# A graph network's node update at the end: products in column and row halves of TensorE's array

## The reference, cut to what matters

```python
h = relu(layernorm(x))
message = relu(concat(h[src], h[dst], edge) @ msg_W1 + msg_b1) @ msg_W2 + msg_b2
agg = segment_sum(message, dst)
x = x + relu(concat(agg, h) @ upd_W1 + upd_b1) @ upd_W2 + upd_b2      # the node update
```

## Time and profile before

| | |
|---|---|
| median of 3 runs | 3957.04 us (3954.34 to 3957.98) |
| the profiled execution's own time | 3974.8 us |
| its span | 3973.0 us |
| TensorE busy, whole span | 2800.8 us (70%) |
| mean granted TensorE clock | 0.769 |
| node update, from its first product (3936.58) to the span's end | 36.4 us |

### The profile page before, as it was taken

One profiled execution on the slowest core, in us unless ns is written; L12 is line 12 of the kernel. 1 busy time (PEld: TensorE's weight loads), 2 busy tenths in 40 slices (PEclk: granted clock), 3 DMA queues, 4 the chain that ended last, 5 costly groups with the idle time before them and its releaser, 6 DMA issues.

```text
span 3973.0 us, 102120 instructions
## 1 busy us (share of the span) xinstructions
PE 2800.8 (70%) x37635; PEld 2380.6 (60%) x37635; DVE 1621.9 (41%) x4904; ACT 1292.0 (33%) x3188; POOL 1478.0 (37%) x1462
## 2 busy tenths in 40 slices
PE   2457777677784777777777777777777777777778
PEld 2335555555563666666666666666666666666666
DVE  8735544444556333333333333333333333333333
ACT  0135555454563222222222222222222222222222
POOL 0654444333424334333333333333333333333331
PEclk6668888787886777877777777777777777777778
DMA  1000000000002122112211121221122112112211
GB/s 44 19 18 16 16 16 16 15 15 15 16 10 52 40 40 42 39 38 41 40 39 41 39 40 39 41 40 39 38 42 40 39 39 42 39 38 42 39 39 38
DMA packets 365051, 133.31 MB, mean 34 GB/s; under 512 B 312657, under 2 KB 342455, under 8 KB 364919
## 3 DMA queue, kind: packets, MB, share of 16 engines
q1 hardware_dynamic: 320248, 85.81, 9.9%
q0 software_dynamic: 44672, 45.83, 6.5%
HBM read 123.94 MB, written 7.54 MB: 33 GB/s over the span
## 4 chain that ended last, share of the span: by engine, by line
PE 67%; issue 23%; DVE 5%; another core or an unknown queue 4%; ACT 1%; DVEq 0%; POOL 0%; DMA 0%; PEldq 0%; ACTq 0%; SPq 0%; POOLq 0%
PE psum L1662 13%; PE psum L1651 12%; PE psum L1717 11%; PE psum L1519 7%; PE psum L1551 7%; PE psum L1641 7%; PE psum L1675 3%; PE psum L1699 3%; PE psum L1540 2%; PE psum L1530 1%; ACT hT L1286 1%; DVE Z L957 1%; PE psum L1485 0%; DVE work L834 0%
## 5 line engine op out<-in xcount | busy, mean ns | idle before, releaser
L673 POOL DMA_INDIRECT rows<-a_rows,idx x980 | 973.2, 993 | 1717.8 <-DMA idx<-src_by_tile 1432.9
L1651 PE MATMUL psum<-wb,eoT 128*64 128x64 f32 x6272 | 502.9, 267 | 461.4 <-issue 451.7
L1651 PEld LDWEIGHTS psum<-wb,eoT 128*64 128x64 f32 x6272 | 371.8, 170 | 571.5 <-issue 569.8
L1286 ACT ACTIVATE hT<-psum 128x392 bf16<-128x392 f32 x1152 | 518.8, 503 | 500.6 <-PE psum L1551 285.6
L1662 PE MATMUL psum<-Y,Z 128*128 128x64 bf16 x8820 | 526.4, 235 | 162.5 <-issue 162.4
L673 POOL DMA_INDIRECT rows<-g_rows,idx x416 | 411.7, 990 | 550.4 <-DMA idx<-src_by_tile 430.7
L1551 PE MATMUL psum<-Z,lo_hi 128*128 128x392 f16 x1152 | 419.5, 380 | 259.7 <-issue 169.7
L1662 PEld LDWEIGHTS psum<-Y,Z 128*128 128x128 bf16 x8820 | 465.2, 126 | 219.3 <-issue 200.2
L1519 PE MATMUL psum<-work,hT 128*128 128x192 bf16 x3528 | 513.6, 269 | 15.9 <-issue 13.2
L1356 ACT ACTIVATE Y<-psum 128x512 f16<-128x512 f32 (+1 forms) x392 | 150.0, 435 | 1151.1 <-PE psum L1699 1147.7
L1374 ACT ACTIVATE Y<-psum 128x384 bf16<-128x384 f32 (+1 forms) x588 | 255.6, 439 | 769.6 <-remote 580.9
(11 more groups left out here) (273 smaller groups left out, 2344.7 us busy)
## 6 DMA issues: line engine op xcount, KB each, us to landing
work<-in_edge_attr_dram SPq DMA_DIRECT2D x392, 128.0 KB
Z<-slot_code SPq DMA_DIRECT2D x196, 96.0 KB
rows<-a_rows,idx POOLq DMA_INDIRECT x980
rows<-g_rows,idx POOLq DMA_INDIRECT x416
idx<-src_by_tile SPq DMA_DIRECT2D x197, 2.5 KB, 1.7
wb<-b_rows SPq DMA_DIRECT2D x196, 16.0 KB
g_rows<-Y SPq DMA_DIRECT2D x1, 1600.0 KB, 7.1
a_rows<-Y SPq DMA_DIRECT2D x6, 256.0 KB, 2.3
```

The costliest lines, as they stand in the source:

```text
L673: pool.indirect_dma_start(out=rows[:, k, t, :], out_offset=None, in_=table, in_offset=bass.IndirectOffsetOnAxis(ap=idx[:, k, t:t + 1], axis=0)
L1286: nc.scalar.activation(counts[:, j % 2, :, t * SLOTS:(t + 1) * SLOTS], psum[:, t % 4, 0:KEYS].rearrange("p (h m) -> p h m", m=SLOTS), ACT.Copy
L1651: TT.matmul(psum[half:half + D, 2 + k % 2, t * D:(t + 1) * D], eoT[:, k % 2, t, half:half + D], wb[:, k, :], start=(t == 0), stop=False)
```

## The change

Chunks of 512 nodes are taken in pairs. The hidden features of an even chunk are computed only into rows 0 to 63, those of an odd chunk only into rows 64 to 127, in the same bank; each product uses 64 columns of the weights. The four products of a pair are written as: `w_node` for the even chunk, `w_node` for the odd, `w_agg` for the even, `w_agg` for the odd. ScalarE writes 64 rows by 512 nodes for each chunk. The second products contract the 64 rows that hold the chunk's hidden features, with the unhalved `w_upd2`; a block of the even chunk (rows 0 to 63) and one of the odd (rows 64 to 127) stand in turn, and they write to two different banks. VectorE reads both banks in one instruction. `w_out` and the instruction that made it go. Semaphores rise once for each pair on TensorE. The order is hidden 0, 1, and then in turn one pair of hidden calls two ahead and one pair of output calls, so three hidden pairs stand before the first output.

```diff
-        w_out = sb("w_out", [P, D])
...
-                V.tensor_tensor(Y[:, c:c + m, :], psum[:, 4 + (c // T) % 2, 0:m * D].rearrange("p (b d) -> p b d", d=D),
-                                X[:, c:c + m, :], ALU.add).then_inc(s_u3c, 1)
+                banks = slice(4 + 2 * ((c // T) % 2), 6 + 2 * ((c // T) % 2))
+                if m == T:
+                    V.tensor_tensor(Y[:, c:c + m, :].rearrange("p (a b) d -> p a b d", a=2),
+                                    psum[:, banks, 0:T // 2 * D].rearrange("p a (b d) -> p a b d", d=D),
+                                    X[:, c:c + m, :].rearrange("p (a b) d -> p a b d", a=2), ALU.add).then_inc(s_u3c, 1)
...
-            nc.scalar.activation(w_out[:, :], w_upd2[:, :], ACT.Copy, scale=0.5).then_inc(s_wTc, 1)
...
-                act.wait_ge(s_u2, q + 1)
-                nc.scalar.activation(acc[:, c:c + m], psum[:, q % 4, 0:m], ACT.Relu, bias=b_upd1[:, :]).then_inc(s_u2c, 1)
+                half = slice(q % 2 * D, q % 2 * D + D)
+                act.wait_ge(s_u2, q // 2 + 1)
+                nc.scalar.activation(acc[half, c:c + m], psum[half, (q // 2) % 4, 0:m], ACT.Relu, bias=b_upd1[half, :]
+                                     ).then_inc(s_u2c, 1)
...
-            pe.wait_ge(s_wTc, 7)
+            pe.wait_ge(s_wTc, 6)
...
+            def half_of(q):
+                return slice(q % 2 * D, q % 2 * D + D)
+
+            def hidden(pair):
+                chunks = [(q, min(512, NP - q * 512)) for q in (2 * pair, 2 * pair + 1) if q * 512 < NP]
+                if pair >= 4:
+                    pe.wait_ge(s_u2c, 2 * (pair - 3))
+                for weights, from_, first in ((w_node, hT, True), (w_agg, acc, False)):
+                    for q, m in chunks:
+                        ins = TT.matmul(psum[half_of(q), pair % 4, 0:m], weights[:, half_of(q)], from_[:, q * 512:q * 512 + m],
+                                        start=first, stop=not first)
+                ins.then_inc(s_u2, 1)
+
+            def output(pair):
+                if pair >= 2:
+                    pe.wait_ge(s_u3c, pair - 1)
+                pe.wait_ge(s_u2c, min(2 * pair + 2, -(-NP // 512)))
+                for b in range(HB):
+                    for q in (2 * pair, 2 * pair + 1):
+                        n = q * HB + b
+                        if n < NB:
+                            ins = TT.matmul(psum[:, 4 + 2 * (pair % 2) + q % 2, b * D:(b + 1) * D],
+                                            acc[half_of(q), n * P:(n + 1) * P], w_upd2[half_of(q), :], start=True, stop=True)
+                ins.then_inc(s_u3, 1)
+
+            hidden(0)
+            hidden(1)
+            for pair in range(NPAIR):
+                if pair + 2 < NPAIR:
+                    hidden(pair + 2)
+                output(pair)
```

More of the change, by code:

```diff
@@ L1250, in _ @@
                 dve.wait_ge(s_u3, c // T + 1)
-                V.tensor_tensor(Y[:, c:c + m, :], psum[:, 4 + (c // T) % 2, 0:m * D].rearrange("p (b d) -> p b d", d=D),
-                                X[:, c:c + m, :], ALU.add).then_inc(s_u3c, 1)
+                banks = slice(4 + 2 * ((c // T) % 2), 6 + 2 * ((c // T) % 2))
[3 more added lines that the diff above has]
+                                    X[:, c:c + m, :].rearrange("p (a b) d -> p a b d", a=2), ALU.add).then_inc(s_u3c, 1)
+                else:
+                    V.tensor_tensor(Y[:, c:c + m, :], psum[:, banks.start, 0:m * D].rearrange("p (b d) -> p b d", d=D),
+                                    X[:, c:c + m, :], ALU.add).then_inc(s_u3c, 1)
         @block.scalar
@@ L1739, in _ @@
             HB = 512 // P
[L1741 to L1758, removed]
@@ L1760, in _ @@
-            hidden(0)
[L1761 to L1766, removed]
+            NPAIR = -(-NB // T)
+            def half_of(q):
[9 more added lines that the diff above has]
+                ins.then_inc(s_u2, 1)
```

## The result

The changed kernel takes 3928.82 us (median of 8 runs, 3911.85 to 3935.99) where the kernel before takes 3949.88 (8 runs, 3941.86 to 3960.15): ratio 0.9948, 95% interval 0.9932 to 0.9965, faster by some 21 us (13.8 to 27 by the interval). I had forecast 3945.3 in a range from 3939 to 3955: the sign is right, the time lies outside the range.

What follows compares the result with a forecast made beforehand. TensorE's own work bounds the node update: first products 13.22, second 5.67 and switches 1.8 make 20.7 us against 32.4, 11.7 less. From the median 3957.04 that gives 3945.3, range 3939 to 3955.

Steps and rivals of the forecast that it cites:

- C: Rival (0.07), node update: halves don't run together with 512 fp32 columns, switches come on top; 1.3 us more, 3958.3.
- D: Rival (0.03), node update: granted clock falls; at half all the way the passes double, 7.2 us more than now, 3964.2.
- the slots: First products: passes start in order, one per half at a time, so n passes take n/2 + 1 slots; 13.22 us.
- My own check: Edge loop, line 1651: n/2 + 1 slots give 17 x 0.054 = 0.92 us against 0.93 measured.
- Second products: Output stages: loads of lower and upper 64 rows overlap; 16 passes take 9 slots, 0.95 us; pairs 0 to 5, 5.67.
- B: Rival (0.24), second products: the row halves' loads don't overlap, 1.68 us a pair; 4.4 us more, 3949.7.
- Switches: TensorE in the node update: 9 changes between column and row halves at 0.2 us, 1.8 us in all, bounds 0 to 2.3.
- A: Main case (0.60), node update: both overlaps hold; 3945.3 us, with bounds 3941.8 to 3945.8.
- The cover: Node update: ScalarE stays hidden behind TensorE, and VectorE's late start is covered by 1.8 us.
- E: Rival (0.06), edge loop: moved buffers and shorter ScalarE code lengthen TensorE's waits; at 5%, 3967.9; against: three runs within 3.6 us.
- a drift of the loop: Range: A's and B's 3941.8 to 3949.7, widened by some 3 us on one side, 5 on the other.
- My sign for E: Profile after: up to 3936 us it should be as before; a shift there is E, or its opposite.

Runs made afterwards that it cites:

- the kernels that undo the placement: Two kernels: the one before with w_out behind all other buffers, ratio 0.9998; the changed one with w_out, its copy and wait put back, 3926.29 us, ratio 0.9957.

## Why the prediction was right and wrong

- **What bounds it, right.** TensorE alone set the update's end, and still does. Rivals C and D did not happen: the passes overlap, and the clock was 1.00 throughout in all three profiles of the changed kernel. (Where the update began at half clock in other runs, one of them was the kernel before.)
- **First products: the slots were mis-sized.** "I take it that a pass starts no earlier than the one before it" failed. I had 13.22 us for all of them; measured are 5.37 + 3 x 1.87 + 1.01 = 11.99 with the switches in them. A stage of 8 passes takes 4 slots and a switch, since TensorE starts the other half's pass ahead of three waiting ones. My own check, 0.92 against 0.93 for line 1651, was luck. In the trace of the kernel before the single passes of that line start two by two, 0.003 us apart, every 0.058 us, from the first pair on; one look at that pair shows it:

```profile
3926.95 0.23 PE L1651 MATMUL psum<-wb,eoT 128*64 128x64 f32 x2
```

So the 0.93 was 16 slots of 0.058 and not 17 of the 0.054 that I had scaled from wider passes. The bound of 4 slots was in the working and was the truth.
- **Second products, right in kind.** Loads of the two row halves overlap, as I took from the column halves; B did not happen. 8 slots of 0.112 and a switch make the 1.04; I had 0.95 and 0.2.
- **Switches, right in size:** 0.15 us each instead of 0.2. With the slots the update took 18.1 us and not 20.7: 14.3 us saved, not 11.7, inside A's own bounds.
- **The cover held:** no wait for ScalarE or VectorE that lengthened the chain. TensorE was faster than I had it, and VectorE's slack of 1.8 us shrank to 0.1 (its first add ended at 3898.9, the loads of output 2 began at 3899.05); with closer outputs it is gone.
- **The time, wrong, by 16.5 us** (3945.3 to 3928.8). Of this 2.6 is the slots. 7.2 is the base: I took the median of three runs, 3957.04, while eight runs have 3949.88. The other 6.7 is the part of the first timing's 21 us that is not the update. It is no more than these runs can be off by: the interval, 0.9932 to 0.9965, holds 14.3 us (0.9964), two repetitions gave 11.8 us (ratio 0.9970 of 3943) and 15.5, and the kernels that undo the placement showed no such effect. That it was scatter of the loops is what these numbers suggest; it is not shown, since the first timing can't be taken apart.
- **The step that failed** for the time is "the three runs lie within 3.6 us" under E, and with it the 3 to 5 us for "a drift of the loop" in the range. Single executions of the kernel before lie 37.5 us apart on one chip (3922.98 to 3960.5), and the medians of two chips are 34 us apart (3943.18 and 3977.09). The profiled execution's 3974.8, which I carried along as a difference that the change leaves alone, is above all 35 runs of the one chip and among the 30 of the other (3967.83 to 3987.21); it probably came from a chip like the second. Either way it was the warning, and a range of 16 us around the median of three runs was too narrow. My sign for E, a shift of the profile ahead of the update, came up with 48.6 us and was no sign: in the three profiles of the one changed kernel the update begins at 3887.9, 3909.8 and 3955.3.

## What to carry to other kernels

Where half of TensorE's array does something twice, two half-array streams side by side took little more than half the time of the stage here: 1.87 us instead of 3.44 for first products, 1.04 instead of 1.68 for second ones, switches included, and nothing at all was gained where both streams used the same half. Turns by product were enough for fp32's two passes, and so were runs of four passes (column halves); with runs of eight (row halves) half of the overlap was lost. Each change between column and row halves cost 0.15 us, so stages may be short. And a gain of 0.4% in a straight stretch is read from the chain of that stretch: the median of three whole runs was off by half of the gain, and two chips differed by more than twice the gain.

## What the runs showed of the hardware

**The same program needs 2172 us on one chip and 3943 or 3977 on two others**, and each variant ran near the pace of its chip. The rows of the costliest wait in the edge loop, changed kernel on a slower chip, then the order with fewer switches on the faster (busy, mean ns, idle before):

```profile
L1657 PE MATMUL psum<-wb,eoT 128*64 128x64 f32 x6272 | 513.3, 267 | 482.1 <-issue 475.2
```

```profile
L1657 PE MATMUL psum<-wb,eoT 128*64 128x64 f32 x6272 | 215.7, 222 | 0.0
```

Windows within the same loop, in the same order:

```profile
1300.00:3800.00 2500.00, 1830.25 (x29338) 1640.53 (x29338) 872.52 (x2762) 687.60 (x1843) 912.77 (x923) 0.77 0.20 40
```

```profile
1300.00:2100.00 800.00, 798.95 (x19605) 765.02 (x19602) 565.94 (x1846) 439.81 (x1231) 612.08 (x617) 1.00 0.40 84
```

On the faster chip TensorE never stops and the granted clock is 1.00; on the others it stops again and again, mostly for 0.2 to 0.5 us between passes and now and then for 1, for nothing that the profile shows, and the clock is 0.77 on the mean. By the starts of this line a superblock takes 13.8 us there and 6.5 on the faster chip. The last three superblocks, which are written out and not in the hardware loop, start 6.01 and 4.51 us apart in profiles from every chip, and the node update has its full pace on all of them. What makes the stops I did not find out; here it explains why the scatter sits in the loops, and that the gain of some 14 us is 0.4% on the one and 0.6% on the other.

**The clock at the update's start.** In four of the profiles (the one shown above and all three from the faster chip) it was granted at or near half for the first few us of the update, in the other nine not. It cost 1.6 to 1.8 us, in kernels of either kind. The thinner work just ahead does not tell them apart. The first profile of the kernel before, which kept its full clock, was as thinly busy in the 7.2 us ahead of the update, 4.11 us against 4.09 above:

```profile
3929.30:3936.50 7.20, 4.11 (x118) 3.66 (x114) 1.40 (x5) 1.38 (x4) 0.00 (x0) 1.00 0.01 2
```

What does tell them apart stays open.

**Halves of the array.** The Trainium skill (TensorEngine Tiling, Key Properties) has a change of mode drain TensorE; the trace agrees, at 0.15 us, and the loads of the new mode start only behind the slot of the old one's last pass (they stand idle for 0.81 us). The list in the Trainium skill (TensorE: Matmul & The Clock Gate, The mechanism) lets a weight load overlap running products only where the row group differs; the text above the list allows a background weight buffer too. By the trace the list is too narrow: with column halves, in the same rows, 8 passes with their loads ran in 4 slots.
